# An attention pass with a hand-written slot order: side work, early loads and the row maxima's transpose are moved

## The reference

```python
x = x + attn(layernorm(x))      # q, k, v = y @ Wq, y @ Wk, y @ Wv; rope(q), rope(k)
                                # softmax(q k^T / 4, causal) v, 4 query heads per key head; @ Wo
x = x + ffn(layernorm(x))       # (silu(y @ Wg.T) * (y @ Wu.T)) @ Wd.T, 512 -> 1376 -> 512
```

## Time and profile before

| | |
|---|---|
| median of 3 runs | 800.17 us (799.15 to 800.98) |
| the profiled execution: its time | 799.32 us |
| its span, first to last instruction | 797.6 us |
| mean granted TensorE clock | 0.985 |
| busy: PE, PEld, DVE, ACT, POOL | 760.5, 507.8, 444.0, 343.6, 211.3 us |
| phase 1 | up to about 390 us |

### The profile page before, as it was taken

How to read it: one execution, slowest core, us unless ns; L and a number is a source line. 1 busy time by engine, 2 the same in 40 slices (tenths; PEclk the granted TensorE clock), 3 DMA queues, 4 the chain that set the end, 5 groups by cost and what they waited for, 6 DMA issues and landing times.

```text
span 797.6 us, 12117 instructions
## 1 busy us (share of the span) xinstructions
PE 760.5 (95%) x4209; PEld 507.8 (64%) x4240; DVE 444.0 (56%) x984; ACT 343.6 (43%) x684; POOL 211.3 (26%) x384
## 2 busy tenths in 40 slices
PE   4699999999999998999799999999999999999998
PEld 3545544554445443454588887888878888788886
DVE  7787888788877786996344543223322243231212
ACT  3427767766877776668533222111121111121111
POOL 3326763477446753334300000000000000000000
PEclk9959999999999999899999999999999999999999
DMA  7437777224423436470296101412005120030001
GB/s 263 110 89 247 211 240 216 68 85 121 116 78 101 120 90 198 125 208 29 90 257 177 55 14 44 141 43 65 27 1 169 42 79 26 0 106 0 1 1 53
DMA packets 74613, 81.84 MB, mean 103 GB/s; under 512 B 8720, under 2 KB 58384, under 8 KB 74352
## 3 DMA queue, kind: packets, MB, share of 16 engines
q1 hardware_dynamic: 73264, 79.98, 32.9%
q10 hardware_dynamic: 1296, 1.18, 0.6%
HBM read 57.02 MB, written 33.36 MB: 113 GB/s over the span
## 4 chain that ended last, share of the span: by engine, by line
PE 50%; DVE 0%; issue 0%; DVEq 0%
PE bank L1495 35%; PE ps_y L1547 15%; PE bank L1534 1%; DVE x_in L1477 0%; DVEq L1476 0%
## 5 line engine op out<-in xcount | busy, mean ns | idle before, releaser
L734 ACT ACTIVATE probs<-ps_t 128x512 f32<-128x512 f32 (+1 forms) x352 | 185.8, 562 | 92.4 <-PE ps_t L1145 91.5
L869 DVE CUSTOM_DVE_ANT_0 ps_s<-ps_s,mask_row 128x512 f32<-128x512 f32 (+1 forms) x240 | 144.7, 643 | 30.3 <-PE ps_s L1113 30.2
L1452 DVE TENSOR_TENSOR h<-h,bank 128x512 f32<-128x512 f32 (+1 forms) x44 | 30.2, 687 | 218.7 <-PE bank L1495 217.5
L1113 PE MATMUL ps_s<-k_rows,q_rows 96*128 96x256 bf16 (+3 forms) x512 | 134.5, 316 | 8.3 <-DMA q_rows<-scratch_q_parts 3.4
L1145 PE MATMUL ps_t<-q_rows,k_rows 98*128 98x512 bf16 (+1 forms) x352 | 127.5, 366 | 6.7 <-DMA q_rows<-m_t 3.1
L1113 PEld LDWEIGHTS ps_s<-k_rows,q_rows 96*128 96x128 bf16 x512 | 44.3, 100 | 87.9 <-issue 34.3
L1390 ACT ACTIVATE h<-bank 128x512 f32<-128x512 f32 (+1 forms) x44 | 26.4, 599 | 149.1 <-PE bank L1495 149.1
L642 POOL TENSOR_SCALAR_AFFINE_SELECT probs<-probs 128x512 f32<-128x512 f32 x128 | 84.6, 661 | 0.0
L1158 PE MATMUL ps_o<-probs,v_ones 128*32 128x512 f32 (+3 forms) x1024 | 82.6, 441 | 0.2 <-ACT o_sb L744 0.2
L1396 ACT CAST h_hi<-h 128x512 fp32r<-128x512 f32 (+1 forms) x44 | 27.3, 620 | 128.5 <-DVE h L1452 128.5
L873 DVE TENSOR_REDUCE m_raw<-ps_s 128x2 f32<-128x512 f32 (+3 forms) x112 | 73.0, 676 | 16.1 <-PE ps_s L1118 14.2
(11 more groups left out here) (154 smaller groups left out, 1357.2 us busy)
## 6 DMA issues: line engine op xcount, KB each, us to landing
scratch_o<-o_sb SPq DMA_DIRECT2D x31, 256.0 KB, 2.4
q_rows<-scratch_q_parts SPq DMA_DIRECT2D x32, 192.0 KB
x_in<-in_x SPq DMA_DIRECT2D x16, 256.0 KB, 4.9
q_rows<-scratch_q_parts SPq DMA_DIRECT2D x32, 128.0 KB
x_res<-in_x SPq DMA_DIRECT2D x16, 256.0 KB, 2.8
o_in<-scratch_o SPq DMA_DIRECT2D x64, 64.0 KB
inverse<-scratch_inverse SPq DMA_DIRECT2D x64, 64.0 KB
out<-x_in SPq DMA_DIRECT2D x16, 256.0 KB, 2.1
```

The costliest lines, as they stand in the source:

```text
L734: nc.scalar.activation(probs[:, g % 2, heads * u:heads * (u + 1), CHUNK_AT[c]:CHUNK_AT[c + 1]], ps_t[:, pos % S_BANKS, 0:heads * CHUNK_N[c ...
L869: nc.vector.tensor_tensor_reduce(out=bank, in0=bank, in1=mask_row[:, T - width:T], scale=1.0, scalar=LOWEST, op0=ALU.add, op1=ALU.max, acc ...
L1113: mm = nc.tensor.matmul(bank[:, place], q_rows[r][0:ROWS, j, P * q:P * (q + 1)], k_rows[r][0:ROWS, 0:width], start=(place == 0), stop=mask ...
L1452: nc.vector.tensor_tensor(h[0:m, r], h[0:m, r], bank[units["up", f] % BANKS][0:m, :], ALU.mult).then_inc(h_ready, 1)
```

## The change

- `max_low` comes after the second bank of slot i = 0, no longer after the first.
- `m_parts` gets 128 columns; 96 of them are zeros, written once by a memset at the start. `transposed_max` so has a stationary operand of 128 columns and writes 128 rows.
- At (0, 3) the dense piece comes ahead of `transposed_max`.
- VectorE's other work moves to slots with i = 2 or 3: `rotated_low` 1 and 4 from slots 13 and 25 to 14 and 26, `xt_low` 2 from 29 to 30, the statistics from 8 to 11 to 6, 7, 10, 11, the means from 12 to 14, the normalising from 18 to 21 to 18, 19, 22, 23, the reciprocal from 16 to 18.
- The load of Wo and the loads for tiles 0 and 1 move from batch 3 to batch 2: slot 1 (Wo), slots 2 and 6 (eight DMAs and one residual tile each). Tiles 2 and 3 are loaded in slots 10 and 14 of batch 3 instead of 8 and 12.

```diff
-LO_SLOT = {7: 0, 13: 1, 15: 2, 22: 3, 25: 4}
-NEXT_XT = {26: 0, 27: 1, 29: 2, 31: 3}
+LO_SLOT = {7: 0, 14: 1, 15: 2, 22: 3, 26: 4}
+NEXT_XT = {26: 0, 27: 1, 30: 2, 31: 3}
-X_SLOT, STATS_SLOT, MEAN_SLOT, APPLY_SLOT = 26, 8, 12, 18
-SUMS_SLOT, INVERSE_SLOT = 7, 16
+X_SLOT, MEAN_SLOT = 26, 14
+STATS_AT, APPLY_AT = {6: 0, 7: 1, 10: 2, 11: 3}, {18: 0, 19: 1, 22: 2, 23: 3}
+SUMS_SLOT, INVERSE_SLOT = 7, 18
-WO_HI, WO_LO, O_LOAD, CTX_SCALE, CTX_HI, CTX_LO = 2, 4, 0, 5, 6, 7
+WO_HI, WO_LO, O_LOAD, CTX_SCALE, CTX_HI, CTX_LO = 2, 4, 2, 5, 6, 7
+WO_LOAD, FIRST_O_LOAD = 1, 2
-        m_parts = sb("m_parts", [P, 2, 2, GROUP, TT], BF16)
+        m_parts = sb("m_parts", [P, 2, P // (GROUP * TT), GROUP, TT], BF16)
...
-            def prepare_batch_0(slot):
-                if slot == 0:
+            def prepare_first_tiles(slot):
+                if slot == WO_LOAD:
+                    sp.wait_ge(inverse_stored, DMA)
                     sp.wait_ge(raw_copied, 13 * DMA)
                     sp.dma_start(to.wo[1][:].bitcast(F32), ...).then_inc(wo_loaded, DMA)
-                    load_residual(sp, d, to, 0, 0)
-                    load_residual(sp, d, to, 0, 1)
+                for t in range(2):
+                    if slot == FIRST_O_LOAD + TT * t:
+                        load_o(sp, d, to, 0, t)
+                        load_residual(sp, d, to, 0, t)
+            def prepare_batch_0(slot):
...
+                    if b == B - 2:
+                        prepare_first_tiles(slot)
...
-                        others.insert(0, lambda: max_low(n + 1))
+                        others[0:0] = [lambda: None, lambda: max_low(n + 1)]
...
+            nc.vector.memset(m_parts[:, :, 2:], 0.0)
...
-                nc.tensor.matmul(to[0:2 * GROUP * TT, 0:P], m_parts[:, n % 2].rearrange("p w j q -> p (w j q)"),
+                nc.tensor.matmul(to[:, 0:P], m_parts[:, n % 2].rearrange("p w j q -> p (w j q)"),
...
+                        for place, kind, k, piece in pieces.get((slot, j), ()):
+                            dense(b + 2 if has_next and kind == "T" else b + 1, kind, k, UNIT0[b] + place, piece)
                         if (i, j) == (0, GROUP - 1) and n + 1 < GROUPS:
                             transposed_max(n + 1)
-                        for place, kind, k, piece in pieces.get((slot, j), ()):
-                            dense(b + 2 if has_next and kind == "T" else b + 1, kind, k, UNIT0[b] + place, piece)
```

More of the change, by code:

```diff
@@ L474, in prepare_batch_0 @@
                 t = (slot - O_LOAD) // TT
-                if slot == O_LOAD + TT * t and t < TT:
-                    if t >= 2:
-                        sp.wait_ge(to.ctx_lo_ready, t - 1)
+                if slot == O_LOAD + TT * t and 2 <= t < TT:
+                    sp.wait_ge(to.ctx_lo_ready, t - 1)
                     load_o(sp, d, to, 0, t)
@@ L919, in next_work @@
                 if b + 2 < B:
-                    if 0 <= slot - STATS_SLOT < TT:
-                        work.append(lambda: layernorm_stats(b + 2, slot - STATS_SLOT))
+                    if slot in STATS_AT:
+                        work.append(lambda: layernorm_stats(b + 2, STATS_AT[slot]))
                     if slot == MEAN_SLOT:
                         work.append(lambda: layernorm_mean(b + 2))
-                    if 0 <= slot - APPLY_SLOT < TT:
-                        work.append(lambda: layernorm_apply(b + 2, slot - APPLY_SLOT))
+                    if slot in APPLY_AT:
+                        work.append(lambda: layernorm_apply(b + 2, APPLY_AT[slot]))
                     if slot in NEXT_XT:
@@ L1124, in transposed_max @@
                     bank_free(PRE_UNITS - 1, 0)
-                    to, ready = ps_d, dense_ready
+                    to, ready = ps_d[:], dense_ready
                 else:
```

## The result

The changed kernel takes 803.06 us (median of 22 runs, 797.68 to 807.58) against 800.35 us for the kernel before (22 runs, 797.77 to 802.11): ratio 1.0027, 95% interval 1.0014 to 1.0040, so 2.7 us slower, a third of a per cent. 802.8 us was forecast. The profiled execution of the changed kernel took 805.55 us, with a span of 803.8 us and a mean clock of 0.974 (before: 799.32, 797.6 and 0.985).

What follows compares the result with a forecast made beforehand. TensorE bounds most phase 1 groups, SyncE's queue some group starts; phase 2 is unchanged. Terms -7.2 - 0.8 + 4.6 + 1.2 + 3.2 + 3.4 - 3.8 + 2.0 = +2.6 us gave 802.8 us, range 796 to 808.

Steps and rivals of the forecast that it cites:

- The narrow transpose: Transpose of the maxima at (0, 3): 128 columns save 0.30 us at each of 24 places, -7.2 us.
- `max_low`'s later place: VectorE reaches `max_low` one bank later: costs nothing, or up to 0.3 us each in seven groups, +2 at most.
- VectorE's other work: Side work leaving slots i = 0 and 1 removes some TensorE waits for row maxima: -0.8 us (0 to -2).
- T1 and T3: Transposes in slots 26 and 30, batches 0 and 1, wait longer for `xt_low`: +4.6 us (+2.4 to +6).
- rival C: Longer stops in slot 26 also bring the clock down; one such fall gives 806.2 us; chance 0.15.
- The start of group 19: Early loads in batch 2, slot 6 delay SyncE: TensorE stops for +3.2 us, half clock after adds +3.4.
- Rival A: Group 19 does not stop, so neither stop nor half clock comes: 796.2 us; chance 0.18.
- rival B: Group 19 stops but the clock holds afterwards: 799.4 us; chance 0.20.
- Group 25: With the loads gone from batch 3, the wait for the maxima there goes: -3.8 us (-3.0 to -4.4).
- Tile 3: Batch 3: its loads now follow the feed-forward weights, VectorE waits some 2.5 us: +2.0 us (0.5 to 3.5).
- Rows just in time: Groups 3, 5 and 11: faster TensorE or later stores make it wait for landing rows: +1.2 us (0 to +2).
- Rival D: The wide transpose stays as slow as the narrow one, losing the 7.2 us: 810.0 us; chance 0.07.

Runs made afterwards that it cites:

- the two one-part kernels: Kernel before with only the 128 columns and memset, 797.08 us; kernel before with only the new order and `max_low`'s later place, 32 columns, 794.68 us.
- max_low_only: Kernel before with `max_low` after the second bank and nothing else; 797.58 us, ratio 0.9968.
- best: Changed kernel with tile 1 loaded in batch 3, slot 2, tile 3 ahead of the feed-forward weights, `xt_low` ahead of `rotated_low`; 786.35 us.
- after_tile3_first: Changed kernel with tiles 2 and 3 loaded in slots 8 and 12 of batch 3 again, ahead of the feed-forward weights; 796.91 us.
- after_xt_first: Changed kernel with `xt_low` 2 back in slot 29 and `xt_low` 0 ahead of `rotated_low` 4 in slot 26; 794.80 us.
- only_loads: Kernel before with only the early loads, and tiles 2 and 3 loaded two slots later; 802.21 us, ratio 1.0028.
- after_tile1_late: Changed kernel with tile 1's loads in batch 3, slot 2, Wo and tile 0 staying early; 796.53 us.
- only_wide: Kernel before with the row maxima's part alone: 128 columns, dense piece ahead of the transpose, `max_low` after the second bank; 790.59 us.
- only_transposes: Kernel before with only `rotated_low` 4 moved to slot 26 and `xt_low` 2 to slot 30; 808.35 us, ratio 1.0089.

## Why the prediction came out right, and where it was wrong

The total was right (+2.6 forecast, +2.7 measured), and the stops stood where the forecast put them. Several sizes were off, and that the total fits to 0.1 us is luck: it left out half clock at three places and was too low for tile 3, it left out a gain at the maxima, and it meets a median that lies between runs with much and runs with little half clock. In the profiled run the same terms come to +6.5 us.

- **The narrow transpose.** 0.97 us against 0.98 forecast, and 0.28 to 0.45 us saved at 23 of the 24 places (that in group 19 runs at half clock): right. The 0.31 us had been put down to the width alone; the two one-part kernels give 0.18 to 0.25 of it to the width and the rest to the order. The Trainium skill (TensorEngine Tiling (Array Packing), Key Properties) has a drain at a change of tiling mode; the width's 0.18 to 0.25 us are what it could explain. The 0.06 us that the order brings with 128 columns it does not, for no mode changes there.
- **`max_low`'s later place** was costed at nothing, up to +2 us. This step failed in sign: alone it is -3.2 us in the medians (max_low_only, 95% interval -1.1 to -4.1), and 0.95 us at each of groups 6 and 14. The step looked at when the maxima would be late and not at what stood behind `max_low` on VectorE in its old place, a bank that was ready.
- **VectorE's other work** was -0.8 us; alone it gives -2.2, and beside `max_low`'s new place about nothing.
- **T1 and T3.** Waits of 2.0 and 1.4 us forecast, 1.90 and 1.42 measured: against the 0.91 us before, 2 x 2.4 = +4.8 us where +4.6 was forecast. What the sum left out is the clock: rival C, with a chance of 0.15, had this fall once, and the profiled run has it twice, for another 3.6 us.
- **The start of group 19.** +6.6 us forecast for stop and half clock, 17.15 - 10.48 = 6.7 measured against best. The stop was longer than forecast (3.93 against 3.2 us), and SyncE lost 1.1 us on one issue of 1.53 us just before. The same issue took 1.29 us in after_tile3_first and 1.26 in after_xt_first, with stops of 3.77 and 3.50, and 0.42 in only_loads with a stop of 2.51. Rival A is refuted. In only_loads the stop was followed by full clock, which is rival B.
- **Group 25.** -3.8 us forecast, -4.6 in the ledger.
- **Tile 3** was the most mis-sized term: +2.0 us forecast, 15.89 - 10.47 = +5.4 measured. The load landed at 358.7, not at 356.5: 4.3 us after its last issue ended, where 2.8 had been taken from the maxima's DMA. VectorE waited 3.22 instead of 2.5 us, and the sum had no half clock behind this stop.
- **Rows just in time** were +1.2 us. In the changed kernel TensorE waits 0.27 us for them at group 3 and 0.60 at group 5. Up to groups 3, 5 and 11 it takes 10.83, 11.03 and 10.48 us, 1.3 us more than three ordinary groups; before it was 0.2 more. So +1.1 us: right.
- **Rival D** is refuted.

**Why the profile says +6.2 and the median +2.7.** The runs of the changed kernel differ in their mean clock: nine of them had 0.972 to 0.976 and a median of 804.6 us, eight had 0.981 to 0.983 and a median of 799.8. A difference of 0.007 in mean clock over 803 us is 5.6 us of full-speed time lost, and these medians are 4.8 apart. So my reading is that the half clock behind T1, group 19 and tile 3 comes in some executions and not in others, and the median sits between; the forecast's +2.6 counted half clock behind one of four such stops. I have the clocks of the runs and not a profile of each, so this is the reading that fits them, and it is not shown. It cannot be all of the spread. The kernel before has none of these stops, only that at group 25, and on the chip of after_tile1_late nine of its runs had a clock of 0.981 and a median of 801.5 us, three had 0.985 and 799.0. And half clock in the first 60 us lasted 17 to 24 us by the profiles; 6.8 us more of it lower the mean clock by 0.004. Such stretches at the start, from the kernel before, the changed kernel and only_wide:

```profile
20.00:60.00 40.00, 32.77 (x146) 19.12 (x146) 32.71 (x67) 13.92 (x25) 12.21 (x12) 0.79 0.38 99
20.00:60.00 40.00, 34.04 (x150) 20.26 (x149) 33.89 (x70) 14.96 (x26) 12.01 (x12) 0.74 0.41 99
20.00:60.00 40.00, 34.25 (x143) 20.87 (x142) 33.77 (x65) 13.20 (x21) 11.26 (x11) 0.70 0.38 99
```

That group 19 costs more in the whole than in only_loads is a stop 1.4 us longer and the half clock behind it. Of the 1.4 us the long issue is 1.1; the last rows also took 3.52 us from issue to release, where it was 3.15.

**What stays open.** The length of the stop alone does not say whether the clock falls: behind 1.90 us at T1 it fell in the changed kernel and in only_transposes, and not in after_tile1_late and after_tile3_first, each time in both batches; behind tile 3 it fell after 2.42 and 2.50 us and held after 2.95. Nor did I find what makes some DMA issues two or three times as long, or why one of 1.26 to 1.53 us stands at the same place, just ahead of the loads of slot 6, in the changed kernel and the three with one part undone and not in best.

## What to carry to other kernels

Before an item is moved in an engine's order, look at what stands ready behind it in the old place: here a small instruction that waited for another engine held up a full PSUM bank, and moving it by one bank gave back 0.95 us where nothing else stood in the way, in all 3.2 us against the wider operand's 3.7 in the medians. When a queue's free time is used for early loads, count every issue that now stands ahead of the next due transfer, and put a stop that TensorE may have at two prices, with and without the half clock behind it. A change with several parts that comes out near zero is worth taking apart: here its good half was worth 14 us, and three small moves undid it.

## What the runs showed of the hardware

- The width of the stationary operand alone changed the distance around a product of 128 moving columns by 0.25 us between bf16 neighbours and dense products (1.28 and 1.03 us), and by 0.18 us behind a dense piece (1.15 and 0.97 us).
- The granted clock fell to half behind stops of 1.90 us in two kernels and held behind the same stops in two others; behind tile 3 it held after 2.95 us. In the kernel before the one stop followed by half clock had 3.06 us.
- The same eight loads and the two residual tiles took SyncE 6.4 us to issue in one run and 8.2 in another; single issues on its queue took 0.36 to 1.86 us, the longest in only_transposes.
